# A decoder layer on one core: score matmuls moved from 96-row stacks to one 32-row strip per head, with one pool of PSUM banks, a folded MLP, a norm per unit and a new prologue

## What is computed

```python
# self-attention, low-rank; k_eff and v_eff are products of the weights
c_kv = x @ W_dkv.T                      # 64 wide
q = (x @ W_dq.T @ W_uq.T).reshape(B, T, 16, 8)
q_lat = einsum('bqhd,hdl->bhql', q, k_eff)
attn = softmax(where(causal, q_lat @ c_kv^T / sqrt(8), -inf))
y = einsum('bhql,hld->bqhd', attn @ c_kv, v_eff)
x = layernorm(x + y)
# attention over [context, x]: 512 + 256 keys, causal in the last 256
q = x @ Wq ; k, v = split(concat(ctx, x) @ Wkv)
x = layernorm(x + softmax(mask(q k^T / sqrt(8))) v @ Wout + bout)
# MLP with a scalar network of 16 hidden values for each of 64 features
s = x @ Win + bin_                      # 64 wide
h = relu(s[..., None] * W1 + b1)        # 64 x 16
out = (einsum('btmh,mh->btm', h, W2) + b2) @ Wout + bout
x = layernorm(x + out)
```

## Time and profile before

| | |
|---|---|
| median of 3 runs | 309.76 us (308.98 to 311.21) |
| profiled execution, span from first to last instruction | 309.5 us |
| what the page gives of time around the span | nothing: the span is 0.3 us under the median |
| instructions | 6148 |
| DMA | 23.64 MB, mean 76 GB/s |

### The profile page before, as it was taken

The page is one execution under the profiler, slowest core; times in us unless marked ns, Lnnn a source line. Parts: engine busy times, 40 slices in busy tenths (PEclk is TensorE's granted clock), DMA queues, the critical chain, the costliest instruction groups (busy, mean ns, idle before and its releaser), DMA issues.

```text
span 309.5 us, 6148 instructions
## 1 busy us (share of the span) xinstructions
PE 277.4 (90%) x2240; PEld 181.3 (59%) x2240; DVE 234.5 (76%) x540; ACT 174.3 (56%) x365; POOL 72.6 (23%) x108
## 2 busy tenths in 40 slices
PE   4918678899999999999999999999999999999762
PEld 3706566576776657665656565665665666554431
DVE  2797716587775998888889878799778799777463
ACT  1520235456556567756667566776676658667430
POOL 8996601001202020301111211013101112112211
PEclk9985969999999999999999999999999999999795
DMA  6669999302034512120006200033000000000001
GB/s 188 243 190 303 258 300 229 137 3 55 4 124 85 175 35 102 54 103 3 1 2 162 48 1 2 1 86 71 2 3 2 2 2 1 3 2 17 2 18 34
DMA packets 16109, 23.64 MB, mean 76 GB/s; under 512 B 1648, under 2 KB 11824, under 8 KB 15952
## 3 DMA queue, kind: packets, MB, share of 16 engines
q1 hardware_dynamic: 13632, 14.19, 16.4%
q0 software_dynamic: 2160, 7.47, 8.0%
q10 hardware_dynamic: 288, 1.59, 1.4%
HBM read 13.02 MB, written 9.96 MB: 74 GB/s over the span
## 4 chain that ended last, share of the span: by engine, by line
PE 72%; DVE 17%; DMA 3%; issue 3%; SPq 1%; ACT 1%; POOL 0%; POOLq 0%; ACTq 0%; DVEq 0%
PE psum L1122 15%; PE psum L1104 13%; PE psum L1067 9%; PE psum L1075 7%; DVE pmax L869 5%; PE psum L1077 4%; PE psum L1130 4%; PE psum L1106 4%; DVE w2x L821 3%; DMA qm<-shift_rows 3%; PE psum L1084 3%; PE psum L1108 2%; DVE nmax_s L880 2%; DVE nmax_s L881 2%; PE psum L1159 1%
## 5 line engine op out<-in xcount | busy, mean ns | idle before, releaser
L735 ACT ACTIVATE probs<-psum 128x512 f32<-128x512 f32 x224 | 127.1, 594 | 61.0 <-PE psum L1104 36.1
L869 DVE TENSOR_REDUCE pmax<-psum 128x1 f32<-128x512 f32 (+2 forms) x176 | 111.9, 682 | 19.6 <-PE psum L1067 10.4
L1104 PE MATMUL psum<-qm,ks 98*128 98x512 f32 x176 | 79.9, 463 | 0.0
L1122 PE MATMUL psum<-probs,v 128*9 128x256 f32 (+1 forms) x1024 | 60.6, 354 | 0.0
L1075 PE MATMUL psum<-ks,qm 96*128 96x128 f32 (+1 forms) x256 | 51.0, 309 | 8.2 <-DVE probs L810 8.2
L1067 PE MATMUL psum<-ks,qm 96*128 96x512 f32 x128 | 52.6, 424 | 0.0
L1075 PEld LDWEIGHTS psum<-ks,qm 96*128 96x128 f32 x256 | 43.1, 202 | 13.1 <-issue 9.6
L866 DVE TENSOR_REDUCE nmax<-psum 128x2 f32<-128x512 f32 (+1 forms) x48 | 31.8, 687 | 18.4 <-PE psum L1077 18.3
L1104 PEld LDWEIGHTS psum<-qm,ks 98*128 98x128 f32 x176 | 33.1, 191 | 17.5 <-ACT probs L735 13.3
L669 POOL TENSOR_SCALAR_AFFINE_SELECT probs<-probs 128x512 f32<-128x512 f32 x32 | 19.7, 634 | 96.5 <-ACT probs L735 96.5
L1122 PEld LDWEIGHTS psum<-probs,v 128*9 128x9 f32 x1024 | 21.7, 90 | 31.2 <-issue 9.4
(11 more groups left out here) (133 smaller groups left out, 291.4 us busy)
## 6 DMA issues: line engine op xcount, KB each, us to landing
qm<-scr_q SPq DMA_DIRECT2D x28, 96.0 KB
ks<-scr_k SPq DMA_DIRECT2D x6, 384.0 KB, 4.4
ks<-scr_m POOLq DMA_DIRECT2D x2, 768.0 KB, 7.6
ks<-scr_m SPq DMA_DIRECT2D x2, 768.0 KB, 6.4
ctxT_sb<-ctxT ACTq DMA_DIRECT2D x1, 1024.0 KB, 8.2
scr_m<-probs POOLq DMA_DIRECT2D x2, 512.0 KB, 7.1
qm<-shift_rows SPq DMA_DIRECT2D x64, 4.0 KB
scr_k<-split_k SPq DMA_DIRECT2D x4, 256.0 KB, 2.0
```

Of the source, the lines that this page charges most:

```text
L735: nc.scalar.activation(probs[:, ring % PRING, h:h + nh, q0:T], src, ACT.Exp, scale=SCALE).then_inc(exp_done, 1)
L869: nc.vector.tensor_reduce(pmax[:, t % 2, col:col + nh, part], tile, axis=AX.X, op=ALU.max).then_inc(max_done, 1)
L1104: nc.tensor.matmul(tbank[n % TBANKS], keys, queries, start=True, stop=True).then_inc(scoresT_ready, 1)
L1122: last = nc.tensor.matmul(obank[t % OBANKS][32 * j:32 * j + HS + 1, q0:T], v, probs[:, pv_no[s] % PRING, j, q0:T], start=(kt == 0), stop=( ...
```

## The change

**Strips.** Each head of a group now has its own 32-partition strip: 3 slots x 8 = 24 rows of data (`DATA`), 26 with the shift rows (`ROWS`). No zeros are needed. A score matmul of head j reads partitions 32j to 32j+23 or 32j+25 (rows 0, 32, 64, 96 of the array) and all 128 columns. Queries and keys lie side by side in one tile (`qk`, and `km` for the context).

**Banks of one head.** A bank of scores (`S`, before `max`) holds one head. In both kinds there are 4 banks of own keys, each with two matmuls (128 keys for the first query tile, 256 for the second: 384 columns) and a mask matmul of 256 columns on all 128 rows. Kind 2 has 8 more of 512 context keys. Of `T` (before `exp`) there is a bank for each head and pair of key tiles: 4 in kind 1 (two matmuls of 256 and 128 columns, and the mask matmul), 12 in kind 2 (two matmuls each, 8 banks of 512 and 4 of 384 columns, no mask matmul; POOL masks as before, in two instructions for both tiles). So `S` has 256 banks in place of 224, and so has `T`.

**One pool.** 7 banks serve all but `pv`; the planner names the bank of every stage, and TensorE waits until its former holder has been read.

**The maximum** is split in halves on POOL in place of DVE; DVE has one small reduction left. **The norm** runs once per unit (16 instructions and two DVE operations in place of four times 4 and two). **The MLP**: Win x W1 is folded to 128 x 1024 (`win1`) and W2 x Wout to 1024 x 128 (`wout2`) by POOL in the kernel; `hid` is 8 float32 matmuls of 256 columns with one operation behind each, `mo` is 16 float32 matmuls that accumulate. **Prologue**: the weights of self-attention are folded with the strips' zero columns, so that unit 0's q and k come out in place without DRAM; its rows of ones come from a K=1 matmul. POOL's large memsets go; the rows of ones of the other units come by four DMAs. Unit 0 is then plain float32 in q and k. Units 1 to 7 and the context still go through DRAM, split in halves by POOL, and all their DMAs are on SP's queue.

```diff
-SLOTS = 3
-STACK = HG * SLOTS * HS
-ROWS = STACK + 2
+STRIP = 32
+DATA = SLOTS * HS
+ROWS = DATA + 2
+WIDE = HG * STRIP
...
-SBANKS, TBANKS, OBANKS, MBANKS = 3, 2, 1, 2
-PRING = 8
+BANKS = 7
+PRING = 4
+SPL = 3
+ROWBUFS = 4
...
+def s_banks(t):
+    own = [("own", j, 0) for j in range(HG)]
+    return own if kind(t) == 1 else [("mem", j, qt) for qt in range(QT) for j in range(HG)] + own
+def pairs(t):
+    return [(0, 1)] if kind(t) == 1 else [(0, 1), (4, 5), (2, 3)]
...
+                    if src == "mem":
+                        nc.tensor.matmul(m, strip(tile, j, DATA)[:, g, qt * P:(qt + 1) * P], strip(km[:, b], j, DATA)[:, g, :],
+                                         start=True, stop=True).then_inc(s_ready, 1)
+                    else:
+                        at = 0
+                        for q in range(QT):
+                            keys = (q + 1) * P
+                            nc.tensor.matmul(m[:, at:at + keys], strip(tile, j, DATA)[:, g, q * P:(q + 1) * P],
+                                             strip(tile, j, DATA)[:, g, T:T + keys], start=(q == 0), stop=False,
+                                             skip_group_check=True)
+                            at += keys
+                        blocks = m[:, 0:3 * P].rearrange("p (n k) -> p n k", n=3)[:, 0:3:2, :]
+                        nc.tensor.matmul(blocks, ident_b[:, :], neg[:, :, :], start=False, stop=True,
+                                         skip_group_check=True).then_inc(s_ready, 1)
...
+                    q = strip(tile, j, ROWS)[:, g, 0:T]
+                    for n, kt in enumerate(pairs(t)[p]):
...
+                        last = nc.tensor.matmul(m[:, n * T:n * T + T - q0], keys, q[:, q0:], start=(n == 0),
+                                                stop=(n == 1 and kind(t) == 2), skip_group_check=True)
+                    if kind(t) == 1:
+                        blocks = m[:, 0:3 * P].rearrange("p (n q) -> p n q", n=3)[:, 0:3:2, :]
+                        last = nc.tensor.matmul(blocks, ident_b[:, :], negT[:, :, :], start=False, stop=True,
+                                                skip_group_check=True)
...
+            def open_bank(s):
+                before = before_in_bank[s]
+                if before is not None:
+                    sem_, value = emptied(before)
+                    pe.wait_ge(sem_, value)
+                return bank(bank_of[s])
...
+                    nc.gpsimd.tensor_copy(high.bitcast(F32R), whole).then_inc(hi_ready, 1)
+                    pool.wait_ge(hi_ready, t + 1)
+                    nc.gpsimd.tensor_sub(low, whole, high).then_inc(nmax_split, 1)
...
+                        for k in range(2):
+                            f = 2 * i + k
+                            last = nc.tensor.matmul(m[:, k * T:(k + 1) * T], win1[:, f * P:(f + 1) * P], x2T, start=True,
+                                                    stop=True)
...
+                        for i in range(QT):
+                            for f in range(FG):
+                                last = nc.tensor.matmul(m[:, i * C:(i + 1) * C], hid[:, f, i * P:(i + 1) * P], wout2[:, f, :],
+                                                        start=(f == 0), stop=(f == FG - 1))
...
+            def first(g, start_bank):
+                m = bank(start_bank)
+                nc.tensor.matmul(m[:, 0:T], wq_s[:, g * WIDE:(g + 1) * WIDE], xT_sb[:, 0:T], start=True, stop=True)
+                nc.tensor.matmul(m[:, T:], wk_s[:, g * WIDE:(g + 1) * WIDE], xT_sb[:, 0:T], start=False, stop=False,
+                                 skip_group_check=True)
+                nc.tensor.matmul(m[:, T:], ones_rows[:, :], ones_in[:, :], start=False, stop=True,
+                                 skip_group_check=True).then_inc(first_ready, 1)
```

More of the change, by code:

```diff
@@ L73 @@
[L73 to L93, removed]
-            "late": 560}
@@ L182, in ready, with bank_for, take_bank @@
-        if what == "hidden" and s[2] and n < B - 1:
-            r = max(r, when(("hidden", n, s[2] - 1)) + COSTS["hidden_gap"])
-        return r
-    def emit(s):
-        out.append(s)
+        if what in ("ln1", "wo", "mo") and any(x[0] == "apply" for x in chain):
+            return NEVER
+        return when(*follows[what](*s[1:]))
+    def bank_for(start):
+        k = min(range(BANKS), key=lambda i: (max(bank_at[i], start), bank_at[i]))
+        return k, max(bank_at[k], start)
+    def take_bank(s, start):
+        k, _ = bank_for(start)
+        bank_of[s], before_in_bank[s] = k, holder[k]
+        holder[k] = s
+        return k
@@ L188, in emit @@
+    def emit(s, begin=None):
+        plan.append(s)
         what, n = s[0], s[1]
-        r = ready(s) if what not in ("max", "exp", "pv") else start(s)
         if s in chain:
             chain.remove(s)
-        end = r
-        if what in PE_COST:
-            cost = PE_COST[what]
-            if what == "max":
-                cost += {1: 0, 2: 110, 4: 220}[max_banks(n)[s[2]][2]]
-            elif what == "exp" and kind(n) == 1:
-                cost += 110
-            elif what == "pv" and s[2] == key_tiles(n) - 1:
-                cost -= 213
-            end = run("pe", r - COSTS["latency"], cost)
@@ L302, in schedule, with spl_free @@
+    def spl_free():
+        n = len(spl_order) - SPL
+        return [("put",) + spl_order[n]] if n >= 0 else []
+    done[("q_in", 0)] = COST["start"]
+    chain += list(LATE)
+    maxima = [("S", t, i) for t in range(STEPS) for i in range(len(s_banks(t)))]
+    exps = [("T", t, p, j) for t in range(STEPS) for p in range(len(pairs(t))) for j in range(HG)]
+    pvs = [("pv", t, p) for t in range(STEPS) for p in range(len(pairs(t)))]
     while maxima or exps or pvs or chain:
         now = free["pe"]
[L305 removed]
+        idle = [s for s in chain if s[0] not in MISC and ready(s) <= now + COST["slack"]]
@@ L306, in schedule @@
         if idle:
-            emit(idle[0])
+            emit(min(idle, key=ready))
             continue
-        best = [(NEVER, 0, 0, None)]
-        for k, s in enumerate(chain):
-            if s[0] == "late":
-                due = COSTS["start"] + COSTS["late_from"] + COSTS["late_gap"] * LATE.index(s[1:])
-                best.append((max(now, ready(s), due), 0, k, s))
-            elif s[0] in MISC:
-                best.append((max(now, ready(s)), MLP_RANKS[s[1]] if s[0] in MLP and s[1] < B - 1 else 0, k, s))
@@ L336, in schedule @@
+        others = [s for s in chain if s[0] not in MISC and ready(s) < NEVER]
+        if best:
+            soon = [x for x in best if x[0] <= now + COST["slack"]]
+            pick = min(soon, key=lambda x: x[1:3]) if soon else min(best, key=lambda x: x[:3])
+            waiting = [s for s in others if ready(s) < pick[0]]
+        else:
+            waiting = others
+        if waiting:
+            s = min(waiting, key=ready)
             emit(s)
             continue
-        waiting = [s for s in chain if s[0] not in MISC and ready(s) < pick[0]]
```

1554 lines of the change are left out of this document (699 added, 855 removed).

## The result

| | before | after |
|---|---|---|
| median | 310.49 us (4 runs, 308.98 to 316.29) | 529.61 us (4 runs, 527.87 to 537.16) |
| span of the profiled execution | 309.5 us | 526.0 us |

The ratio is 1.706 (95% interval 1.6985 to 1.7138). The forecast was 328 us with a range of 283 to 346: the sign is right and the size is not, 202 us short.

The account below looks back on a forecast made before the run. TensorE was taken to bound the kernel. From 309.5 us, own-key banks, other switches, MLP and tail added, while context banks, T of kind 2, start and waits subtracted, giving 328.2, said as 328 us; range 283 to 346.

Parts of the forecast that it names:

- Switches cost, masks pay twice: The forecast itself: strips change the array's division and each mask pays twice; 328 us, 313 to 345, chance 0.56.
- Own-key banks: Two strip matmuls, a 128-row mask and switches: 0.55 us a bank; +25.6 us in S, +16.5 in T of kind 1.
- What bounds the kernel now: Opening step: TensorE bounds both main stages; its work, priced by distances between starts, sums to 247 of 262 us.
- Context banks: Matmuls of different heads can run side by side: S -14.7 us, T of kind 2 -12 us.
- Start, -17: Prologue: scores from about 15.5 us (-9), less PE idle and lost time (-8); together -17 us, range -8 to -22.
- S of steps 1 to 3 and the products fill PE: In the start: this work removes most of 4.5 us idle and 4 us lost between 40 and 60; -8 us.
- MLP +12.8: MLP goes from 2.7 to 6.9 us per unit, three units in the main stages: +12.8 us, +8 if half falls in waits.
- waits: Kind 2: seven banks remove PE's 13.3 us wait for ACT, static order gives some back; -8 us, -15 to +5.
- everything else: Shift, norm, products and MLP stages on the whole array between strip work pay 0.2 us switches: +14 us, 7 to 20.
- Tail +1.5: Last unit's norm is larger, MLP stretch taken as no different: +1.5 us, range -1 to +6.
- Rival B: 24-row matmuls and 128-row masks mix without emptying the array: 284 us, range 276 to 306, chance 0.33.
- Rival C: The round trip costs and nothing runs side by side: 359 us, or 345 to 362, chance 0.11.

Follow-up runs that it names:

- the run with 24 context rows: Kernel before with its 128 context matmuls of the max stage reading 24 rows in place of 96: 394.1 us.
- The whole-array form: Kernel after with every score matmul on all 128 rows in place of its strip, four heads' scores summed and exp scaled: 370.5 us.
- float32r: Kernel after with unit 0's queries and keys in float32r, one pass in place of two: 493.7 us.

## Why the prediction was right in sign and wrong in size

- **Switches cost, masks pay twice: right, the price too low.** "Own-key banks", 0.36 + 0.2 = 0.55 us. Measured 0.64 for S and 0.58 for T at 2.4 GHz: the switch price was read off `pv`, whose weights have 9 columns. With 128 columns a change adds 0.18 on each side, as the run with 24 context rows shows. The upper bound that I named was 0.65; for 128 S banks and 64 T banks it is some 13 us over 0.55. At 1.2 GHz a change is 0.29 and the masks' place on 128 rows cost 104 us.
- **The clock: the step that failed.** Every price in "What bounds the kernel now" is a distance at 2.4 GHz, and the whole sum is made with them, after a start of some 10 us. No term, bound or rival let the level fall in the main stages. I took it that a busy PE keeps the level, as the earlier trace rows show for the kernel before. After, it did not: 119 to 155 us by the stretches from 80 to 480 us, 142 to 185 with the start. The whole-array form points to the same size from the other side: nearly all at the higher level behind 40 us, 157 us less, with the side-by-side gain lost and the switches saved. Of the 1.04 us of an S bank, 0.4 is the clock.
- **Kind 1** has a step of 10.2 us (163.6 over 16) where I had 6, **kind 2** 15.8 where I had 9 to 10. Strips do run side by side, as "Context banks" had it, but what this saved was not measured by itself, and no stage came out shorter.
- **Start, -17: wrong sign, +39.** Three errors: the foldings and `first` all ran at the 1.2 GHz level, `first` took 3.15 us in place of 2.2, and the first score was at 30.3; unit 0's two-pass score matmuls, which front and diff name, had no term in my sum (21 us of the 57 us by which the first exponential missed the forecast, as float32r shows); and "S of steps 1 to 3 and the products fill PE" was counted as a gain, while these stages stand ahead of the first T in PE's list.
- **MLP +12.8, waits, everything else:** not separable one by one. The whole-array form has them without the masks' switches: kind 1 +10, kind 2 +25 over before, so the sum of these terms (with -8 for waits) was too kind. **Tail +1.5:** +3. From `hid` to `mo` it took 10.5 us, between the 8.2 and 15 worked out:

```profile
510.10 5.67 PE L1019 MATMUL psum<-xT_sb,win 128*128 128x256 f32 x16 [0.52 <-issue]
516.83 3.81 PE L1027 MATMUL psum<-wout,ctxT_sb 128*128 128x128 f32 x32 [1.06 <-DVE ctxT_sb L786]
```

- **PE without idle, DVE 196, ACT 176, POOL 79: right**, and they rule out every explanation by a wait. Rival B's bank (0.36) needs the whole array, which is not this change. Rival C (nothing side by side) is refuted by starts 0.01 us apart.

On clocks the Trainium skill (TensorE: Matmul & The Clock Gate, HAM oscillation) tells of kernels in which waits between matmuls let the clock fall. The trace here shows another way: 40.00 of 40 us busy at 0.50.

**What is still open.** Runs with 24 and 26 rows held the lower level even with two strips at a time, and with the masks in the strips, where strips of several heads overlap in kind 1, it was the lower level for 76 of 93 us too. Yet the clock rose at times between strips, in the kernel after for 37 us from 350 us on. So few occupied rows bring the clock down, but how many strips have to overlap, or how much whole-array work has to lie between them, to keep it was not settled.

## What to carry to other kernels

Read the granted clock as a quantity that a change can move, and not only by idle time: before matmuls are cut to a quarter of the rows, run one kernel with such matmuls in place of the whole ones, which here showed 84 us for a one-line edit. Zeros in the contraction cost no time of their own here (512 columns followed each other after 0.24 us on 72 rows as on 96 and 98); removing them saved nothing on balance, and the strips lost the clock. Price a change of division with weights as wide as the ones that follow it, and keep whole-array work out of a run of strips.

## What the runs showed of the hardware that I had not expected

- TensorE stayed at 1.2 GHz while busy without a gap (0.50 from 120 to 160 us, 40.00 us busy). 72 rows in 128 of the matmuls: 0.952 and 310 us; 48: 0.884 and 368; 24: 0.811 and 394; 24 to 26 in the context and T matmuls of kind 2: 472.7 us and 0.50 from 140 to 420 us.
- Weights of zeros on 98 rows left the clock alone (0.958).
- A change between a strip and the whole array with weights of 128 columns: some 0.18 us at 2.4 GHz and 0.29 at 1.2, each way.
- The recorded clock can't be trusted at the start: it reads 1.00 until its first change, at 84.0 us in the kernel after, at 136.8 us with the masks in the strips, while one `first` (3.15 us for six passes of 256 columns, with gaps), the S banks of unit 0 and a `pv` of 1.40 us have the distances of the lower level. Two other executions of the kernel after give a mean clock of 0.79 against 0.69 of the profiled one, at times 0.3% apart. Distances between starts decide.
